# Attention and a binary feed-forward block on one core: dense pieces dealt to other steps, relu sums joined, constants cast on ScalarE, and the PSUM banks divided 2-3-2

## The chip, the cores and the metric

The kernel runs on one core of one Trainium2 chip. The metric is the device time of one execution in microseconds (us). A core has TensorE (PE, its weight loads are PEld), VectorE (DVE), ScalarE (ACT), GpSimd (POOL) and SyncE (SP), which issues most of the transfers. PE writes into PSUM, which has eight banks of 128 x 512 f32; here seven of them are lent to units of work and the eighth, o_bank, collects the attention output.

## What is computed

The input x is 8 batches of 1024 tokens with 256 channels. Weights and constants of other layers of the reference are left out here.

```python
# attention in windows of (b, n); in the kernel one batch is 1024 tokens, 16 heads of 16 channels
qkv = x @ w_qkv.T + b_qkv
q, k = elu(q) + 1, elu(k) + 1
q, k = apply_rope(q, sin, cos), apply_rope(k, sin, cos)
attn = softmax(q @ k.T * D**-0.5) @ v
attn = attn + depthwise_conv3(v, w_lepe) + b_lepe
h0 = layernorm(x + attn)
# feed-forward, the three kernels are booleans read as +1 or -1
h = relu(s0 * (concat[h0, -h0] @ pm1(k0))) * 2
h = relu(s1 * (h @ pm1(k1))) * 2
out = layernorm(h0 + s2 * (h @ pm1(k2)))
```

## The kernel before, in words

**Steps.** The work is 8 batches (NB), each of 8 pairs of heads (PAIRS), each of 8 blocks of 128 keys (T): 512 steps of one pair and one key block, 64 to a batch (BATCH). In step s, PE computes the scores S of step s + 12 for two heads in two halves (`scores`, L527 to L535: four matmuls into banks), and the transposed scores T of step s (`scores_T`, L537 to L545: four matmuls); S and T of different heads are issued in turns and run side by side on different rows of the array. DVE takes the row maxima of S (`row_max`, L889), ACT takes exp of T (`exp_probs`, L737), and PE multiplies the exponentials of step s - 1 with v (`weighted_v`, L573, 16 matmuls). The maxima of a pair are joined, transposed by PE in the step with kt = 5 ("max rows", L590) and written by SP into the query stack before T of that pair begins. In the step with kt = 2 the attention output of the pair before is transposed ("O rows", L596).

**Dense pieces.** All the rest of PE's work is cut in units that each fill one PSUM bank and that are dealt by hand to steps, in `dealt` (L106): for batch c the projections of q and k ("proj", 4 units each), the bounds of the heads ("scale", 2), the projection of v ("V", 4); for batch m, one batch behind, the transposes of the normed rows ("hT", 2 + 2), the first layer ("L0", 8 + 8 units, two to a step), the second ("L1", 8 + 8 units, each of two pieces in two steps) and the third ("L2", 2 + 2 units, two pieces each). A piece is issued in a step between the two groups of scores. A "scale" unit is eight small matmuls (`head_bounds`, L554): four sums of relu outputs, each used in two products. What does not fit in the steps is done behind them, in the order of END_UNITS (L101).

**Order on ACT and DVE.** Both follow the same table in their own streams. For a step ACT does the two exps of the second head, then what ended at the end of the step before (`done_behind(s - 1)`, for proj), then what ended within this step, then the two exps of the first head, then the ReLU of the hidden unit that ended last in this step (`done_behind(s)`). DVE does the two maxima of the first head of S, then `done_behind(s - 1)`, the max rows, the rest of this step's units, the norm's statistics, and the other two maxima (L1084 to L1121). A hidden unit is read twice, by ACT (the high half in f16, L804) and then by DVE (the low half, L959), and its bank is free after DVE. A proj unit's bank is free after ACT's second read (L782).

**Banks.** `program_order` (L179) hands out banks in rings: a unit takes the next bank of its kind's ring, and PE waits (`wait_free`) until the unit that had this bank before has been read. "O rows" and "max rows" units take a bank of the dense ring as well, ahead of the step's dense pieces. In the first batch the rings are S (0, 1, 4), T (2, 3, 5) and dense (6); from the second batch on S (0, 1), T (2, 3), dense (4, 5, 6).

**The start and the constants.** Before step 0, q and k of batch 0 are projected, rotated, split, written to HBM and read back as stacks, and the maxima of 12 steps are taken (L1041). Then DVE works out the signs and scales of the feed-forward kernels (L1060 to L1069, nine small operations in a chain) and, behind the maxima of steps 0 to 5, casts k0, k1 and k2 from bytes to f16 (`weights`, L1071). The bytes of k1 lie in the tile attn (stage1, L341).

**GpSimd and SP.** POOL does, for each batch in a written order (L1281 to L1308), the normalisation of the attention of each pair, the depthwise convolution (lepe), the elu, rotation and split of q and k of the next batch with their writes to HBM, the scales of the norms and the load of x. SP waits in its order for the max rows, the freed stacks and the scratch, and issues the loads, the stores of the output (L515) and the loads of the edges and of xT (L517).

Of the kernel before, what the change touches and what calls it, by code (L numbers as in the profile page):

```python
# [24 lines left out]
ALU = mybir.AluOpType  # L25
# [75 lines left out]
END_UNITS = [*out_units(TAIL - 1, 1), *hT_units(TAIL, 0), *hT_units(TAIL, 1),  # L101
# [4 lines left out]
def dealt():  # L106
# [9 lines left out]
    for c in range(1, NB):  # L116
        b = (c - 1) * BATCH
        deal(b + Q_AT, proj_units(c, 0))
        deal(b + SCALE_AT[0], [("scale", c, 0)])
        deal(b + K_AT, proj_units(c, 1))  # L120
        deal(b + SCALE_AT[1], [("scale", c, 1)])
        deal(b + V_AT, v_units(c))
    for m in range(NB - 1):
        b = (m + 1) * BATCH
        deal(b + 17, hT_units(m, 0), 2)
        deal(b + 18, hT_units(m, 1), 2)
        deal(b + 19, hidden_units("L0", m, 0), 2)
        if m < TAIL - 1:
            deal(b + 23, hidden_units("L1", m, 0, range(3)))
            deal(b + 33, hidden_units("L1", m, 0, range(3, KF)))  # L130
            deal(b + 47, hidden_units("L0", m, 1), 2)
            deal(b + 51, out_units(m, 0))
            deal(b + 55, hidden_units("L1", m, 1))
            deal(b + 75, out_units(m, 1))
        else:
            deal(b + 23, hidden_units("L1", m, 0))
            deal(b + 39, hidden_units("L0", m, 1), 2)
            deal(b + 43, out_units(m, 0))
            deal(b + 47, hidden_units("L1", m, 1))
# [39 lines left out]
def program_order():  # L179
# [26 lines left out]
    rings = (4, 5, 6, 0, 1, 2, 3)  # L206
# [74 lines left out]
def build(nc, x, xT, wT, b_qk, b_v, w_lepe, b_lepe, cos, sin, k0, k1, k2, s0, s1, s2, out):  # L281
    with ExitStack() as ctx:
# [33 lines left out]
        relu_sum = sb("relu_sum", [P, 4, 2], F32)  # L316
        pow2_q = sb("pow2_q", [P, 1 + H], F32)
# [23 lines left out]
        stage1 = attn[:].rearrange("p t c -> p (t c)").bitcast(U8)  # L341
# [44 lines left out]
        max_split = sem("max_split")  # L386
        scale_made = sem("scale_made")
# [47 lines left out]
        def _(sp):  # L435
# [74 lines left out]
            for n in range(NB * PAIRS):  # L510
# [16 lines left out]
        def _(pe):  # L527
# [26 lines left out]
            def head_bounds(unit):  # L554

                w = unit[2]
                pe.wait_ge(dve_setup, 3)
                units.wait_read(pe, ("proj", unit[1], 2 * w + 1, 1))
                units.wait_free(pe, unit)
                bank = units.out(unit)  # L560
                terms = [(ct, half) for ct in (2 * w, 2 * w + 1) for half in range(2)]
                for ct, half in terms:
                    total = relu_sum[:, ct, half:half + 1]
                    nc.tensor.matmul(bank[:, 0:1], same_head[:], total, start=(ct, half) == terms[0],  # L564
                                     stop=(ct, half) == terms[-1], skip_group_check=True)
                for ct, half in terms:
                    total = relu_sum[:, ct, half:half + 1]
                    done = nc.tensor.matmul(bank[:, 1:1 + H], total.to_broadcast([P, P]), head_mask[:],  # L568
                                            start=(ct, half) == terms[0], stop=(ct, half) == terms[-1],
                                            skip_group_check=True)  # L570
                done.then_inc(units.full_sem(unit), 1)
# [164 lines left out]
        def _(act):  # L736
# [69 lines left out]

            def normalise(m, which, t):
# [24 lines left out]
            for s in range(STEPS):  # L832
# [9 lines left out]
                if kt == 3 and n > 0 and j != 5 and n + 3 < NB * PAIRS:  # L842
                    copy_v(n + 2 if j == 6 else n + 3)
                if kt == 5 and j == 6 and n + 3 < NB * PAIRS:
                    copy_v(n + 3)
# [14 lines left out]
                if b >= 1 and i in NORMALISE_AT[0]:  # L860
                    normalise(b - 1, 0, NORMALISE_AT[0][i] + 1)
                if j == 5 and 3 <= kt < 7 and b + 1 < NB:
# [5 lines left out]
            copy_o_rows(NB * PAIRS - 1)  # L868
            for t in range(T // 2):
                normalise(NB - 1, 0, t)  # L870
            for unit in END_UNITS:
# [9 lines left out]
        def _(dve):  # L881
# [36 lines left out]
            def elu(c, ct):  # L918
# [4 lines left out]
                  .then_inc(elu_done, 1)  # L923

# [91 lines left out]
            for ct in range(2):  # L1016
                elu(0, ct)
            dve.wait_ge(rows_loaded, 7 * 16)
# [3 lines left out]
            def rotated(ins):  # L1022
                ops[0] += 1
                ins.then_inc(start_split, 1)
                if ops[0] in (2, 4):
                    elu(0, 1 + ops[0] // 2)
                dve.wait_ge(start_split, ops[0])
# [13 lines left out]
            for v in range(T + LEAD):  # L1041
                if v == T + 1:
                    split_max_rows(0)
                for h in range(2):
                    for half in range(2):
                        row_max(v, h, half)
                if v == T - 1:
# [310 lines left out]
```

## Time and profile before

| | us |
|---|---|
| median of 3 runs | 2267.48 (2260.52 to 2269.52) |
| profiled execution | 2269.32 |
| its span, first to last instruction | 2267.5 |
| around the span | 1.8 |

| engine | busy us | share of the span |
|---|---|---|
| PE matmul | 2133.7 | 94% |
| DVE | 1685.9 | 74% |
| ACT | 1475.4 | 65% |
| POOL | 913.3 | 40% |

Busy time of PE is modelled from pipelined matmuls, and two matmuls that run side by side count once. Where a step begins can be read from the first of its four matmuls of line L543: a step is four of them, a batch 256.

### The profile page before, as it was taken

What the parts mean: (1) busy time and instruction counts of PE and PEld (TensorE: products, weight loads), DVE (VectorE), ACT (ScalarE), POOL (GpSimd) and SP (SyncE); (2) the same over time, 40 slices, a digit from 0 to 9 for tenths busy, and PEclk for the clock granted to TensorE, in tenths of its full rate; (3) what the DMA queues carried; (4) which work ended last, traced back from release to release, by engine and by line L of the source; (5) the groups of instructions that cost most, each with busy time, mean ns of one, the idle gap of its engine ahead of it and who ended that gap; (6) DMA issues with size and microseconds to landing.
All of it is one profiled execution on the core that took longest, in us unless ns stands there. A gap on an engine that the chain in (4) does not pass through costs nothing.

```text
span 2267.5 us, 43445 instructions
## 1 busy us (share of the span) xinstructions
PE 2133.7 (94%) x17088; PEld 869.2 (38%) x17088; DVE 1685.9 (74%) x3018; ACT 1475.4 (65%) x2845; POOL 913.3 (40%) x522
## 2 busy tenths in 40 slices
PE   4788899999999999999999999999999999899997
PEld 2122323344343444334343443434443343334344
DVE  6957687878787877878777787868778787878243
ACT  3157578766677666866677666776668666776631
POOL 1228608560375406851185603853067601600000
PEclk8579899999999999999999999999999999999999
DMA  5001110011001110012000210011101110010000
GB/s 176 27 8 39 48 45 16 27 52 39 15 9 52 54 32 13 25 45 67 15 15 29 69 39 15 9 52 61 31 9 34 36 48 15 16 34 1 1 19 19
DMA packets 40140, 76.87 MB, mean 34 GB/s; under 512 B 14992, under 2 KB 19456, under 8 KB 36864
## 3 DMA queue, kind: packets, MB, share of 16 engines
q1 hardware_dynamic: 34752, 51.02, 7.9%
q0 software_dynamic: 5184, 23.07, 2.8%
q8 instruction: 135, 2.21, 0.4%
q14 instruction: 69, 0.57, 0.1%
HBM read 46.27 MB, written 25.17 MB: 32 GB/s over the span
## 4 chain that ended last, share of the span: by engine, by line
PE 81%; DVE 13%; ACT 4%; issue 1%; DMA 1%; POOL 0%; SPq 0%; ACTq 0%; POOLq 0%; DVEq 0%
PE unit_banks L656 24%; PE unit_banks L533 20%; PE o_bank L586 20%; DVE maxima L892 9%; PE unit_banks L613 5%; PE unit_banks L669 5%; PE unit_banks L624 3%; ACT probs L745 2%; PE unit_banks L601 1%; PE unit_banks L543 1%; PE unit_banks L564 1%; PE unit_banks L568 1%; DVE h0T L959 1%; ACT rows L812 0%; PE unit_banks L594 0%
## 5 line engine op out<-in xcount | busy, mean ns | idle before, releaser
L892 DVE TENSOR_REDUCE maxima<-unit_banks 128x1 f32<-128x512 f32 x2048 | 1308.6, 685 | 428.9 <-PE unit_banks L533 422.1
L745 ACT ACTIVATE probs<-unit_banks 128x512 f32<-128x512 f32 x2048 | 1116.0, 598 | 665.4 <-PE unit_banks L543 655.1
L533 PE MATMUL unit_banks<-k_stack,q_stack 48*128 48x512 f16 x2048 | 662.2, 394 | 61.8 <-DVE maxima L892 38.3
L543 PE MATMUL unit_banks<-q_stack,k_stack 50*128 50x512 f16 x2048 | 651.2, 389 | 1.9 <-ACT probs L745 1.7
L586 PE MATMUL o_bank<-probs,v_pair 128*32 128x256 f32 x8192 | 570.1, 391 | 3.1 <-issue 3.1
L656 PE MATMUL unit_banks<-h0T,w 128*128 128x512 f16 x2048 | 480.9, 380 | 0.0
L1217 POOL TENSOR_TENSOR attn<-o_rows_sb,rden 128x256 f32<-128x256 f32 x63 | 39.0, 618 | 923.2 <-DVE rden L905 912.6
L533 PEld LDWEIGHTS unit_banks<-k_stack,q_stack 48*128 48x128 f16 x2048 | 154.5, 94 | 597.8 <-DVE maxima L892 300.0
L586 PEld LDWEIGHTS o_bank<-probs,v_pair 128*32 128x32 f32 x8192 | 208.8, 109 | 308.7 <-issue 217.4
L656 PEld LDWEIGHTS unit_banks<-h0T,w 128*128 128x128 f16 x2048 | 186.5, 98 | 228.1 <-issue 38.6
L543 PEld LDWEIGHTS unit_banks<-q_stack,k_stack 50*128 50x128 f16 x2048 | 153.3, 94 | 16.1 <-ACT probs L745 11.4
L613 PE MATMUL unit_banks<-xT_sb,wT_sb 128*128 128x512 f32 x256 | 131.2, 642 | 24.0 <-DMA xT_sb<-in_xT 9.7
L959 DVE SCALAR_TENSOR_TENSOR h1T<-unit_banks,h1T 128x512 f16<-128x512 f32 x128 | 87.4, 683 | 81.5 <-ACT h1T L804 81.5
L1233 POOL TENSOR_TENSOR lepe_tmp<-v_ext,lepe_rows 128x1024 f32<-128x1024 f32 x48 | 113.0, 2354 | 70.6 <-DVE max_rows L913 68.1
L669 PE MATMUL unit_banks<-w,h1T 128*128 128x256 f16 x1024 | 121.2, 273 | 8.0 <-DVE rows L977 8.0
L656 PE MATMUL unit_banks<-hT,w 128*128 128x512 f16 x512 | 122.8, 380 | 4.9 <-DVE h0T L959 4.4
L1189 POOL TENSOR_SCALAR work<-work 128x1024 f32<-128x1024 f32 x26 | 72.0, 2767 | 112.5 <-ACT work L782 111.3
L1235 POOL TENSOR_TENSOR rows<-rows,lepe_tmp 128x1024 f32<-128x1024 f32 x48 | 113.1, 2357 | 3.8
L804 ACT ACTIVATE h1T<-unit_banks 128x512 f16<-128x512 f32 x128 | 77.3, 604 | 52.1 <-PE unit_banks L656 52.1
L669 PEld LDWEIGHTS unit_banks<-w,h1T 128*128 128x128 f16 x1024 | 97.0, 98 | 27.7 <-DVE rows L977 8.9
L959 DVE SCALAR_TENSOR_TENSOR h0T<-unit_banks,h0T 128x512 f16<-128x512 f32 x128 | 86.5, 684 | 11.4 <-ACT h0T L804 10.9
L812 ACT ACTIVATE rows<-rows,shift,rstd 128x256 f32<-128x256 f32 x120 | 71.1, 603 | 20.7 <-POOL shift L1255 20.7
(125 smaller groups left out, 1541.7 us busy)
## 6 DMA issues: line engine op xcount, KB each, us to landing
rows<-in_x POOLq DMA_DIRECT2D x8, 1024.0 KB, 7.6
xT_sb<-in_xT SPq DMA_DIRECT2D x8, 1024.0 KB, 14.2
q_stack<-q_scratch SPq DMA_DIRECT2D x128, 64.0 KB, 2.0
k_stack<-k_scratch SPq DMA_DIRECT2D x128, 64.0 KB, 2.0
out<-rows SPq DMA_DIRECT2D x8, 1024.0 KB, 4.1
q_scratch<-parts POOLq DMA_DIRECT2D x14, 512.0 KB, 3.3
k_scratch<-parts POOLq DMA_DIRECT2D x14, 512.0 KB, 3.3
q_stack<-q_scratch SPq DMA_DIRECT2D x128, 32.0 KB, 1.9
```

Of the source, the lines that this page charges most:

```text
L533: nc.tensor.matmul(units.out(unit), q_stack[row:row + STACK, r, t * P:(t + 1) * P], k_stack[row:row + STACK, r, half * 512:(half + 1) * 51 ...
L543: nc.tensor.matmul(units.out(unit), k_stack[row:end, r, kt * P:(kt + 1) * P], q_stack[row:end, r, half * 512:(half + 1) * 512], start=True ...
L586: done = nc.tensor.matmul(o, v_pair[:, n % RING, kt, h, :], p[:, :, parity, :], start=kt == 0 and half == 0, stop=kt == T - 1, skip_group_ ...
L613: done = nc.tensor.matmul(units.out(unit), wT_sb[:, kc, ct * P:(ct + 1) * P], xT_sb[:, kc, half * 512:(half + 1) * 512], start=kc == 0, st ...
L656: done = nc.tensor.matmul(units.out(unit), w, a, start=k == 0 and i == 0, stop=k == tiles - 1 and i == 1)
L669: done = nc.tensor.matmul(units.out(unit)[:, t * C:(t + 1) * C], h1T[:, a, k, (2 * i + t) * P:(2 * i + t + 1) * P], w2[:, k, :], start=k = ...
L745: nc.scalar.activation(probs[:, 2 * (kt % 2) + h, half * 512:(half + 1) * 512], units.out(unit), ACT.Exp, scale=exp_regs[2 * (n % PAIRS) + ...
L804: done = nc.scalar.activation(dst[:, 0, unit[3], :], units.out(unit), ACT.Relu)
L892: nc.vector.reduce_max(maxima[:, v // T % 2, h * T + t, half:half + 1], units.out(unit), AXIS_X)\
L959: free(unit, nc.vector.scalar_tensor_tensor(dst[:, 1, u, :], s, 0.0, dst[:, 0, u, :], ALU.max, ALU.subtract))
L1233: ins = combine(lepe_tmp[:], v_ext[:, t + tap:t + tap + T // 2, :], row(tap), ALU.mult)
L1235: ins = combine(base, base, lepe_tmp[:], ALU.add)
```

## The change

- `rings` is one setting for all steps: S (0, 1), T (2, 3, 4), dense (5, 6). The ring of the start and of the end is reordered.
- `dealt` has other steps: q at 6 (7 before), scale at 14 (12) and 40 (35), k at 32 (29; 22 for batch 1, its scale at 28), V at 50 (43), hT at 19 and 20 (17, 18), L0 at 22 (19) and 46 (47), L1 of the first half at 26 and 36 (23, 33), L2 at 54 (51), L1 of the second half at 58 for six units and 74 for two (55), L2 at 79 (75). The last L1 unit of batch 6 goes behind the steps (LATE_UNITS).
- DVE sums the four relu sums to one (`join_sums`), and a scale unit is two matmuls instead of eight.
- The scales and w0 are made on DVE ahead of the first maxima; w1 and w2 are cast on ACT, one operation of 128 x 512 at the end of each of steps 8 to 27 (16 for w1, 4 for w2). The bytes of k1 lie in rows[1].
- The copies of v for the pairs, the statistics, the normalisation on ACT, the order on POOL and two steps on SP are moved along.

```diff
-Q_AT, K_AT, V_AT, SCALE_AT = 7, 29, 43, (12, 35)
-STATS_AT = {**{6 + t // 2: (0, t - t % 2) for t in range(0, T, 2)}, 14: (1, 4), 16: (1, 6), 52 + 4: (1, 0), 52 + 6: (1, 2)}
-MOMENTS_AT = {10: 0, 17: 1}
-NORMALISE_AT = ({13: 0, 14: 2, 15: 4, 16: 6}, {20 + t: t for t in range(T)})
-COPY_V_AT = {3: 3}
+Q_AT, V_AT = 6, 50
+K_AT, SCALE_AT = {1: 22}, ({}, {1: 28})
+STATS_AT = {**{6 + t // 2: (0, t) for t in range(0, T, 2)}, 27: (1, 4), 29: (1, 6), 59: (1, 0), 61: (1, 2)}
+MOMENTS_AT = {10: 0, 31: 1}
+NORMALISE_AT = ({13: 0, 14: 2, 15: 4, 16: 6}, {37 + t: t for t in range(T)})
+COPY_V_AT = {3: (0, 1, 2, 3, 4, 7), 1: (7,), 5: (7,)}
+WEIGHTS_AT = 8
...
+LATE_UNITS = [("L1", TAIL - 1, 1, KF - 1), *out_units(TAIL - 1, 1)]
+END_UNITS = [*LATE_UNITS, *hT_units(TAIL, 0), *hT_units(TAIL, 1),
...
-        deal(b + 17, hT_units(m, 0), 2)
-        deal(b + 18, hT_units(m, 1), 2)
-        deal(b + 19, hidden_units("L0", m, 0), 2)
+        deal(b + 19, hT_units(m, 0), 2)
+        deal(b + 20, hT_units(m, 1), 2)
+        deal(b + 22, hidden_units("L0", m, 0), 2)
         if m < TAIL - 1:
-            deal(b + 23, hidden_units("L1", m, 0, range(3)))
-            deal(b + 33, hidden_units("L1", m, 0, range(3, KF)))
-            deal(b + 47, hidden_units("L0", m, 1), 2)
-            deal(b + 51, out_units(m, 0))
-            deal(b + 55, hidden_units("L1", m, 1))
-            deal(b + 75, out_units(m, 1))
+            deal(b + 26, hidden_units("L1", m, 0, range(3)))
+            deal(b + 36, hidden_units("L1", m, 0, range(3, KF)))
+            deal(b + 46, hidden_units("L0", m, 1), 2)
+            deal(b + 54, out_units(m, 0))
+            deal(b + 58, hidden_units("L1", m, 1, range(6)))
+            deal(b + 74, hidden_units("L1", m, 1, range(6, KF)))
+            deal(b + 79, out_units(m, 1))
...
-    rings = {"S": (0, 1, 4), "T": (2, 3, 5), "": (6, 0, 1, 2, 3, 4, 5)}
+    rings = {"S": (0, 1), "T": (2, 3, 4), "": (5, 6, 4, 0, 1, 2, 3)}
...
-    rings[""] = (6,)
+    rings[""] = (5, 6)
...
-        if s == BATCH:
-            rings = {"S": (0, 1), "T": (2, 3), "": (4, 5, 6)}
...
-    rings = (4, 5, 6, 0, 1, 2, 3)
+    rings = (5, 6, 4, 0, 1, 2, 3)
...
-                if j == 3 and b >= 2:
+                if j == 5 and b >= 2:
                     store_out(b - 2)
-                if j == 5 and b < NB - 1:
+                if j == 6 and b < NB - 1:
                     load_edges(b + 1)
...
-                terms = [(ct, half) for ct in (2 * w, 2 * w + 1) for half in range(2)]
-                for ct, half in terms:
...
+                bank, total = units.out(unit), sums[:, w:w + 1]
+                nc.tensor.matmul(bank[:, 0:1], same_head[:], total, start=True, stop=True, skip_group_check=True)
+                nc.tensor.matmul(bank[:, 1:1 + H], total.to_broadcast([P, P]), head_mask[:], start=True, stop=True,
+                                 skip_group_check=True).then_inc(units.full_sem(unit), 1)
...
+                if i < 2 * KF:
+                    k, cols = i // 2, slice(i % 2 * 512, (i % 2 + 1) * 512)
+                    nc.scalar.activation(w1[:, k, cols], k1_u8[:, k, cols], ACT.Identity, bias=s_work[:, 2:3],
+                                         scale=s_work[:, 1:2])
+                else:
+                    k = slice(2 * (i - 2 * KF), 2 * (i - 2 * KF) + 2)
+                    nc.scalar.activation(w2[:, k], k2_u8[:, k], ACT.Copy, bias=-1.0, scale=2.0)
...
+            def join_sums(c, w):
+
+                units.wait_read(dve, ("proj", c, 2 * w + 1, 1))
+                nc.vector.reduce_sum(sums[:, w:w + 1], relu_sum[:, 2 * w:2 * w + 2, :], AXIS_XY).then_inc(sums_joined, 1)
...
                 lepe(b, 7, LEPE_OPS)
+                if b == 0:
+                    normalise_o(n)
                 if b + 1 < NB:
                     elu(b + 1, 0)
-                if b >= 2:
-                    ln_scales(b - 2, 1)
                 normalise_o(n + 1)
...
                 normalise_o(n + 2)
+                if b >= 2:
+                    ln_scales(b - 2, 1)
+                if b > 0:
+                    normalise_o(n + 3)
...
```

## Rows read from the trace of the kernel before

**Rows 1.** The page, part 4: the chain that ended last, by engine.

```profile
PE 81%; DVE 13%; ACT 4%; issue 1%; DMA 1%; POOL 0%; SPq 0%; ACTq 0%; POOLq 0%; DVEq 0%
```

**Rows 2.** Windows of four batches, L543 alone: us, busy (count), PEclk.

```profile
86.40:334.20 247.80, 90.69 (x256) 19.88 (x256) 0.86 0.11 33
334.20:585.80 251.60, 82.65 (x256) 19.64 (x256) 0.99 0.11 32
585.80:848.80 263.00, 79.42 (x256) 19.07 (x256) 1.00 0.11 34
...
1902.50:2154.40 251.90, 80.34 (x256) 18.54 (x256) 1.00 0.05 14
```

**Rows 3.** Windows of steps of batch 2, L543 alone, columns as there.

```profile
634.27:640.01 5.74, 1.22 (x4) 0.30 (x4) 1.00 0.01 3
649.78:655.90 6.12, 2.77 (x8) 0.66 (x8) 1.00 0.20 50
655.90:665.18 9.28, 2.92 (x8) 0.67 (x8) 1.00 0.06 11
706.07:722.10 16.03, 4.88 (x16) 1.18 (x16) 1.00 0.13 35
748.04:755.90 7.86, 2.44 (x8) 0.59 (x8) 1.00 0.19 69
759.83:764.24 4.41, 1.22 (x4) 0.30 (x4) 1.00 0.04 15
```

**Rows 4.** Timeline of PE, step 13 of batch 2: start us, us, what.

```profile
640.57 0.28 PE L594 MATMUL unit_banks<-ident,max_both 128*16 128x128 f32 x1
642.45 1.92 PE L669 MATMUL unit_banks<-w,h1T 128*128 128x256 f16 x16 [1.60 <-DVE rows L977]
```

**Rows 5.** Timeline of DVE, step 13 of batch 2.

```profile
640.44 1.29 DVE L892 TENSOR_REDUCE maxima<-unit_banks 128x1 f32<-128x512 f32 x2 [0.25 <-PE unit_banks L533]
641.64 0.74 DVE L977 SCALAR_TENSOR_TENSOR rows<-unit_banks,s_work,rows 128x512 f32<-128x512 f32 x1
```

**Rows 6.** Timeline of PE, step 21 of batch 2.

```profile
673.90 1.03 PE L656 MATMUL unit_banks<-hT,w 128*128 128x512 f16 x4
675.56 1.04 PE L656 MATMUL unit_banks<-hT,w 128*128 128x512 f16 x4 [0.63 <-DVE h0T L959]
```

**Rows 7.** Timeline of PE, step 50 of batch 2.

```profile
793.47 2.13 PE L656 MATMUL unit_banks<-hT,w 128*128 128x512 f16 x8
```

**Rows 8.** Timeline of PE, a projection in batch 0.

```profile
220.75 1.96 PE L613 MATMUL unit_banks<-xT_sb,wT_sb 128*128 128x512 f32 x4 [2.33 <-ACT h1T L782]
```

**Rows 9.** Windows of L543: batch 0, steps 0-6 and 56-63; batch 1, 0-6.

```profile
86.40:121.50 35.10, 13.91 (x28) 2.62 (x28) 0.61 0.06 16
312.53:334.30 21.77, 10.60 (x32) 2.68 (x32) 1.00 0.10 23
334.30:354.40 20.10, 10.01 (x28) 2.44 (x28) 1.00 0.07 18
```

**Rows 10.** Timeline of DVE at the start, in order of time.

```profile
58.01 19.23 DVE L892 TENSOR_REDUCE maxima<-unit_banks 128x1 f32<-128x512 f32 x32 [7.71 <-PE unit_banks L533]
...
87.64 2.26 DVE L1061 TENSOR_SCALAR s_sign<-s_sign 128x3 f32<-128x3 f32 x1
...
118.68 1.20 DVE L1082 TENSOR_SCALAR w<-rows 128x2048 f16<-128x2048 uint8 x1
```

**Rows 11.** Lines: ACT with scale and bias from tiles.

```profile
L812 ACT ACTIVATE rows<-rows,shift,rstd 128x256 f32<-128x256 f32 x120 | 71.1, 603 | 20.7 <-POOL shift L1255 20.7
```

**Rows 12.** Waits of SP: what, us in total, times, longest.

```profile
SPq L278 <- DMA k_scratch<-parts: 145.2, 7, 24.9
```

**Rows 13.** Timeline behind the last step: PE.

```profile
2157.01 7.15 PE L669 MATMUL unit_banks<-w,h1T 128*128 128x256 f16 x64
...
2168.87 3.53 PE L636 MATMUL unit_banks<-ident,rows 128*128 128x128 f32 x16 [4.71 <-ACT rows L812]
```

**Rows 14.** Window of L543 in batch 3, columns as in rows 2.

```profile
911.40:930.00 18.60, 6.79 (x19) 1.46 (x18) 0.91 0.09 22
```

More of the change, by code:

```diff
@@ L118, in dealt @@
         deal(b + Q_AT, proj_units(c, 0))
[L119 to L121 removed]
+        deal(b + scale_at(c, 0), [("scale", c, 0)])
+        deal(b + k_at(c), proj_units(c, 1))
+        deal(b + scale_at(c, 1), [("scale", c, 1)])
         deal(b + V_AT, v_units(c))
@@ L316, in build @@
         relu_sum = sb("relu_sum", [P, 4, 2], F32)
+        sums = sb("sums", [P, 2], F32)
         pow2_q = sb("pow2_q", [P, 1 + H], F32)
@@ L554, in head_bounds @@
             def head_bounds(unit):
-                w = unit[2]
+                _, c, w = unit
                 pe.wait_ge(dve_setup, 3)
-                units.wait_read(pe, ("proj", unit[1], 2 * w + 1, 1))
+                pe.wait_ge(sums_joined, 2 * c + w + 1)
                 units.wait_free(pe, unit)
-                bank = units.out(unit)
-                terms = [(ct, half) for ct in (2 * w, 2 * w + 1) for half in range(2)]
-                for ct, half in terms:
[L563 to L571, printed above, removed]
+                bank, total = units.out(unit), sums[:, w:w + 1]
+                nc.tensor.matmul(bank[:, 0:1], same_head[:], total, start=True, stop=True, skip_group_check=True)
+                nc.tensor.matmul(bank[:, 1:1 + H], total.to_broadcast([P, P]), head_mask[:], start=True, stop=True,
+                                 skip_group_check=True).then_inc(units.full_sem(unit), 1)
             def weighted_v(s, half):
@@ L841, in _ @@
                     copy_o_rows(n - 1)
[L842 to L845, printed above, removed]
+                if n > 0 and j in COPY_V_AT.get(kt, ()):
+                    ahead = {1: 1, 3: 2, 5: 3}[kt] if j == PAIRS - 1 else 3
+                    if n + ahead < NB * PAIRS:
+                        copy_v(n + ahead)
                 for unit in done_within(s):
@@ L868, in _ @@
             copy_o_rows(NB * PAIRS - 1)
+            high_part(LATE_UNITS[0])
             for t in range(T // 2):
                 normalise(NB - 1, 0, t)
-            for unit in END_UNITS:
+            for unit in END_UNITS[len(LATE_UNITS):]:
                 if unit[0] in HIDDEN:
@@ L1017, in _ @@
                 elu(0, ct)
+            join_sums(0, 0)
             dve.wait_ge(rows_loaded, 7 * 16)
@@ L1026, in rotated @@
                     elu(0, 1 + ops[0] // 2)
+                if ops[0] == 4:
+                    join_sums(0, 1)
                 dve.wait_ge(start_split, ops[0])
@@ L1040, in _ @@
             v_out(("V", 0, 3))
[L1041 to L1047, printed above, removed]
-                    join_maxima(0)
             dve.wait_ge(k_loaded, 6 * 16)
@@ L1095, in _ @@
                         split_max_rows(unit[1])
+                for w, at in enumerate((Q_AT, k_at(b + 1))):
+                    if b + 1 < NB and i == at + 5:
+                        join_sums(b + 1, w)
                 if kt == RECIPROCAL_STEP and n > 0:
@@ L1119, in _ @@
                         join_maxima(v // T)
-                if s < 6:
-                    weights(s)
+            for unit in done_behind(STEPS - 1):
+                dense(unit)
             final, m = NB * PAIRS - 1, NB - 1
@@ L1149, in _ @@
             ln_moments(m, 0)
-            for unit in END_UNITS[:2]:
+            for unit in LATE_UNITS:
                 dense(unit)
-            units.wait_read(dve, END_UNITS[1])
+            units.wait_read(dve, LATE_UNITS[-1])
             normalise(0)
@@ L1156, in _ @@
             ln_moments(m - 1, 1)
-            for unit in END_UNITS[2:]:
+            for unit in END_UNITS[len(LATE_UNITS):]:
                 dense(unit)
@@ L1302, in _ @@
                     rotate_side(b + 1, 1)
-                normalise_o(n + 3)
+                if b == 0:
+                    normalise_o(n + 3)
                 if b + 1 < NB:
                     split(b + 1, 1)
+                normalise_o(n + 4)
+                normalise_o(n + 5)
+                if b + 1 < NB:
                     load_x(b + 1)
-                for k in range(4, PAIRS - 1):
-                    normalise_o(n + k)
+                normalise_o(n + 6)
             ln_scales(NB - 1, 0)
```

43 lines of the change are left out of this document (26 added, 17 removed).

## The prediction, made before the changed kernel ran

> **What bounds the kernel now.** I read the chain first: PE carries 81% of it and DVE 13% [rows 1]. Then I asked how long a batch of 64 steps takes, by counting the 256 matmuls of L543: 263.0 us in batches 2 to 6 (batch 3: 264.6), 251.6 in batch 1, 251.9 in batch 7, 247.8 in batch 0, where the clock was granted to 0.86 only [rows 2]. Then single steps: a step with an L0 or L1 piece takes 3.93 us (7.86 for two), one with a proj or V piece 4.01 (16.03 for four), O rows add 0.48 (4.41), a scale unit adds 1.8 (5.74), a step with no piece takes 3.06, the two hT steps together 9.28 [rows 3]. In the full steps PE is never free, so whatever makes it wait there is paid in full. The question is therefore which waits for a bank the new rings make.
>
> **How a bank wait looks.** PE can begin a piece some 0.5 us into a step. DVE reads what ended with the step before only after two maxima of this step. In step 13 of batch 2 the L2 unit has the bank of the one that ended in step 12: max rows start at 640.57, L2 could start 0.1 later, starts at 642.45 [rows 4], when the residual, issued behind the maxima at 641.64, has been written [rows 5]. That is 1.8 us lost, and with no max rows ahead 1.85. Two more waits of a shorter kind are there: the second L0 unit of a step waits for the second of the step before, 0.83 us in step 21 (second group of four at 675.56, due 0.83 behind 673.90) [rows 6]; in step 50 the pieces take 2.13 instead of 1.90 behind O rows, and the step is 0.43 longer than 3.93 + 0.04 + 0.48 [rows 7]. Without something ahead this kind costs 0.91. A unit behind a proj unit waits for ACT, which does two exps and two activations first: 2.33 us [rows 8].
>
> **What the rings do.** I went through the table of steps with both rings, own units (O rows, max rows) included, and counted the units whose bank is freed only in the very step in which they want it. Before, with three dense banks, a steady batch has 5 (two of them hidden, by the scale unit ahead and in the hT steps). After, with two, it has 23: every O rows or max rows unit that takes a turn hands the next dense unit the bank of the last one. By kind, for batches 2 to 6:
> first piece, step kt = 6 or 3, nothing ahead (steps 6, 14, 19, 30, 38, 46, 62): 7 x 1.83 = 12.8;
> first piece behind O rows (2, 26, 42, 50, 58): 5 x (1.81 - 0.48) = 6.7;
> behind O rows and a proj bank (10, 34): 2 x (2.35 - 0.48) = 3.7;
> V behind V in step 53: 1.8; behind the new scale unit in step 40: 1.4;
> second L0 unit (23, 24, 25, 47, 48, 49): 6 x 0.91 = 5.5; second hT unit (20): 1.3.
> Sum 33.2 us a batch. Batch 1 has 18 (24.3 us), batch 7 has 19 (22.8 us): 152 waits and 213 us in all, 1.40 each. None of them has a cover: PE issues in order, and all that stands behind it are the scores that ACT and DVE wait for.
>
> **What it saves in the steady batches.** Three old waits go: 1.77 + 0.85 + 0.43 = 3.05. Two scale units of eight small matmuls become two: 6/8 of 1.8, twice, 2.7. The sum on DVE (a few tenths, twice a batch) lies beside PE. One of the two empty steps is filled: an empty step takes 3.06 for 2.1 of PE work (3.93 less the piece's 1.83), so 0.95. The hT steps keep 6.4 of PE work out of 9.28 less O rows 0.48: 2.4. Together 9.1; after: 263.0 - 9.1 + 33.2 = 287.1, +24.1 a batch, +120.5 in five, less 1.6 for batch 3's half-clock stretch. Batch 1: -10.6 (three pieces go to later steps, 3.1; scale 4.3; old waits 1.3; hT steps 1.9) + 24.3 = +13.7. Batch 7: one more piece in place of an empty step +0.9, old waits -1.3, hT steps -2.4, new waits +22.8: +20.0.
>
> **Batch 0.** Here PE has room, and one dense bank made each proj and V unit wait for the last. With two banks only V in step 53 does. S loses its third bank: with S on three banks an empty step takes 2.72 (21.77 for 8), on two 2.87 (20.10 for 7) [rows 9]; I take 2.80, since that batch 1 has other work too. w1 and w2 on ACT: an ACT operation with scale and bias from tiles takes 603 ns for 256 columns [rows 11], so some 0.8 for 512; ACT's four exps leave about 0.4 free in a step, 20 steps lose 0.2: 4. Sum: 50 x 2.80 + 4 + 12 x 4.01 + 1.8 + 2 x 3.25 = 200.5. Steps 0 to 6 took 35.1 at a clock of 0.61 [rows 9], and 0.14 of the whole batch's clock was lost [rows 2], which cost at most 35; the new batch keeps PE busier, I take 11 (between 0 and 35). 211.5 against 247.8: -36.3. T's third bank is costed at nothing: ACT was the last to free a T bank in few steps.
>
> **Start.** DVE idles 7.7 us before its first maxima at 58.0, and the constants took it from 87.6 to 119.9 between maxima [rows 10]. The nine small operations and w0 come to 10.4; moved ahead they fill the 7.7 and delay the maxima by 2.7. Their old price is inside batch 0.
>
> **Costed at nothing.** The tail: PE ends L2 at 2164.2 and waits to 2168.9 for the normed rows [rows 13]; the late L1 unit's 3.7 fits in these 4.7. The K chain on POOL starts three steps later; SP waited 20.7 us a batch for the k scratch [rows 12], to about step 44. Now it is step 47, with SP's loads of the max rows that PE asks for in step 48 queued behind; one step is left. If that cover goes, each step of lateness costs 4.5 us in six batches. The store and the edges on SP move by one or two pairs and had a step or more to spare; POOL's norm scales move too, on an engine that is busy 40% of the span.
>
> **Sum.** 120.5 - 1.6 + 13.7 + 20.0 - 36.3 + 2.7 = +119.0 on the span of 2267.5: 2386.5, with 1.8 around it 2388.3. The profiled execution (2269.3) is 1.8 above the median, so against the runs I forecast 2387, 5% slower.
>
> **Rivals.**
> *The clock falls as well.* The trace shows it where PE has light steps in a row: in batch 3 the stretch with steps 16 to 19 has 0.91 of the clock [rows 14], and cost 1.6, in one of six equal batches. The new waits bunch in steps 19 to 26 and 46 to 50, where a fifth to a quarter of PE's time is idle; against it, batch 0's empty steps, 2.72 for 2.1 of work, ran at 1.00 [rows 9]. Four such falls a batch in seven batches at 1.6: +45, 2432. Chance 0.14. The Trainium skill (TensorE: Matmul & The Clock Gate, A second HAM failure mode: psum-queue depth-cycling) says that a matmul stream that cycles through PSUM banks and idles briefly between groups makes the clock swing between its two levels; by that rule this is the likelier outcome, but the trace has it once in six batches.
> *Not slower: the bank waits shrink.* If DVE and ACT, rested by the first waits, free the banks sooner, each may cost what the cheapest one did, 0.43: 152 x 0.43 = 65 against savings of 94 (213 - 119), 2240. It decides below 94/152 = 0.62 each. Against it: the two maxima of the same step stand ahead of the read in DVE's stream, however rested it is [rows 5]. Chance 0.04.
> *A second buffer is enough.* With all waits hidden the sum is 2269.3 - 94, 2175. Speaks for it: nothing but that two banks suffice when units are read within a step. Chance 0.01. The Trainium skill (TensorE: Matmul & The Clock Gate, HAM oscillation — how this bites in real kernels) tells of a kernel in which double-buffering PSUM gave no further gain; by that the number of dense banks would hardly matter. The 1.8 us of step 13 say otherwise here.
> *The K chain is late.* Two steps late in six batches, +54 on top: 2441. Chance 0.03. *The sum of scale units is left as it was* (the compiler does not drop anything here, but the four relu sums might be late for join_sums): +2.7 a batch, inside the range.
>
> **Numbers.** Forecast 0.76, clock 0.14, K chain 0.03, not slower 0.05, elsewhere 0.02. A measurement of this kernel can tell 0.5% (11 us) from no change. Faster 0.05, within 0.01, slower 0.94. Range: the low end has waits 15% cheaper (-32) and batch 0 without any clock loss (-11), with a little for both: 2340. The high end takes in the clock's case: 2435.
>
> **What would show it.** Steady batches of 287 us by the count of L543; in them steps 6, 30, 38, 62 at 5.8 and steps 23 to 25 at 4.8, with PE released by DVE's L959 or L977; scale steps at 0.45 above the piece; proj steps of batch 0 at about 4.0; DVE with no gap before the first maxima and ACT casting in steps 8 to 27. I am wrong if a batch stays at 263 or below, if PE's waits for DVE or ACT ahead of dense pieces stay below 100 us in all, or if batch 0 does not shrink.

## The result, and the profile after

The changed kernel takes 2442.82 us (median of 4 runs, 2431.28 to 2448.98), the kernel before 2266.13 beside it. The ratio is 1.078, with a 95% interval of 1.073 to 1.082. The profiled execution, the longest of the four, has a span of 2447.2. The forecast was 2387 with a range of 2340 to 2435: the direction holds and so do the waits for banks, but the median lies 8 us above the range, and most of what is missing is a second cause, the clock of TensorE. Of all the executions below one, of the run read_first, took 5119.74 us where its other nine took 2255.87 to 2268.51; nothing on record says why, and the ratios leave it out.

The chain that ended last, by engine and by line, in the changed kernel:

```profile
PE 76%; DVE 19%; ACT 2%; issue 2%; DMA 1%; SPq 0%; POOL 0%; ACTq 0%; POOLq 0%; DVEq 0%
PE unit_banks L660 23%; PE unit_banks L545 20%; PE o_bank L590 19%; DVE maxima L911 13%; PE unit_banks L673 5%; PE unit_banks L617 5%; PE unit_banks L628 2%; DVE h1T L983 2%; DVE h0T L983 1%; ACT probs L749 1%; PE unit_banks L555 1%; PE unit_banks L640 1%; DVE hT L980 0%; ACT work L786 0%; DVE rows L1001 0%
```

PE has gone from 81% of the chain [rows 1] to 76%, and DVE from 13% to 19%. Lines are numbered anew: S is L545, T is L555, the dense pieces L660 and L673, the low half on DVE L983. Next, who waits for whom (us in total, times, longest us); these groups were small or absent before:

```profile
PEld unit_banks L660 <- DVE h1T L983: 81.8, 48, 2.0
...
PE unit_banks L660 <- DVE h1T L983: 69.5, 47, 1.7
PEld unit_banks L660 <- DVE h0T L983: 62.9, 49, 1.7
...
PE unit_banks L660 <- DVE h0T L983: 40.9, 49, 1.5
```

PE itself (not its weight loads, which wait over the same time) now stands 69.5 + 40.9 us before pieces of L1 and L0 until DVE has read a bank, 96 times, and the modelled ends of matmuls hide a part of each wait. Now the batches, as in [rows 2], from batch 0 on with 5, 6 left out (window, us, busy and count of L555, PEclk):

```profile
90.63:298.83 208.20, 93.18 (x256) 21.64 (x256) 0.96 0.13 38
298.83:565.63 266.80, 82.44 (x256) 19.72 (x256) 0.99 0.10 30
565.64:864.76 299.12, 80.61 (x256) 18.73 (x256) 0.96 0.10 30
864.77:1159.46 294.69, 79.93 (x256) 18.83 (x256) 0.98 0.10 31
1159.47:1458.59 299.12, 80.71 (x256) 18.82 (x256) 0.96 0.10 30
2052.46:2326.70 274.24, 80.24 (x256) 18.36 (x256) 0.99 0.04 12
```

Batch 0 is 39.6 us shorter. Batches 1 and 7 are 15 and 22 longer, and batches 2 to 6, which took 263.0, take 294.7 to 299.1. In these the clock stands at 0.96 to 0.98, where it had been 1.00 (0.99 in batch 3 for one fall). Single steps of batch 4 (steps 2, 23 to 25, 30, 34 and 38):

```profile
1167.32:1173.06 5.74, 1.22 (x4) 0.29 (x4) 1.00 0.01 3
1265.42:1280.05 14.63, 3.71 (x12) 0.89 (x12) 1.00 0.20 63
1297.67:1305.04 7.37, 1.29 (x4) 0.31 (x4) 0.77 0.01 1
1316.99:1324.93 7.94, 1.65 (x4) 0.32 (x4) 0.79 0.01 2
1336.88:1342.62 5.74, 1.22 (x4) 0.29 (x4) 1.00 0.02 4
```

Step 2 takes 5.74 for 4.41, steps 23 to 25 take 4.88 each for 3.93, step 38 takes 5.74: at full clock these are the waits of the prediction, 1.33, 0.95 and 1.81. Step 30 is of the same kind as 38, and step 34 is a wait behind a proj unit in a step with O rows, priced at 6.36; but they take 7.37 and 7.94, at a clock of 0.77 and 0.79. That is the part that was not in the sum. All falls of batches 1 to 7 begin in steps with a wait for a bank (6, 10, 14, 19, 30, 34, 38, 62). One plain wait, step 38, in the timeline (start us, us, what):

```profile
1336.78 0.60 ACT L808 ACTIVATE h1T<-unit_banks 128x512 f16<-128x512 f32 x1
...
1337.31 1.29 DVE L911 TENSOR_REDUCE maxima<-unit_banks 128x1 f32<-128x512 f32 x2 [0.25 <-PE unit_banks L545]
1337.34 1.08 ACT L749 ACTIVATE probs<-unit_banks 128x512 f32<-128x512 f32 x2
...
1338.52 0.68 DVE L983 SCALAR_TENSOR_TENSOR h1T<-unit_banks,h1T 128x512 f16<-128x512 f32 x1
...
1339.26 1.90 PE L660 MATMUL unit_banks<-h0T,w 128*128 128x512 f16 x8 [1.75 <-DVE h1T L983]
```

ACT writes the high half of the L1 unit at 1336.78, before this step's maxima are even begun. DVE takes the two maxima until 1338.6 and only then reads the unit. The new unit could have begun at 1337.5, where PE's idle time starts, and begins at 1339.26.

### The profile page after: what moved, and what is told of

Read it like the earlier page. It is cut to its first block, busy times and chain, and to the rows that moved or that the text cites. A ratio compares the mean times of both kernels' runs of the same rounds, so it can differ in the third digit from the quotient of the medians.

```text
span 2447.2 us, 43069 instructions
## 1 busy us (share of the span) xinstructions
PE 2166.0 (89%) x16896; PEld 851.5 (35%) x16896; DVE 1683.0 (69%) x3029; ACT 1491.5 (61%) x2865; POOL 913.2 (37%) x522
## 4 chain that ended last, share of the span: by engine, by line
PE 76%; DVE 19%; ACT 2%; issue 2%; DMA 1%; SPq 0%; POOL 0%; ACTq 0%; POOLq 0%; DVEq 0%
PE unit_banks L660 23%; PE unit_banks L545 20%; PE o_bank L590 19%; DVE maxima L911 13%; PE unit_banks L673 5%; PE unit_banks L617 5%; PE unit_banks L628 2%; DVE h1T L983 2%; DVE h0T L983 1%; ACT probs L749 1%; PE unit_banks L555 1%; PE unit_banks L640 1%; DVE hT L980 0%; ACT work L786 0%; DVE rows L1001 0%
## 5 line engine op out<-in xcount | busy, mean ns | idle before, releaser
L545 PE MATMUL unit_banks<-k_stack,q_stack 48*128 48x512 f16 x2048 | 671.1, 397 | 58.2 <-DVE maxima L911 29.7
L555 PE MATMUL unit_banks<-q_stack,k_stack 50*128 50x512 f16 x2048 | 658.0, 392 | 1.2 <-ACT probs L749 1.2
L660 PE MATMUL unit_banks<-h0T,w 128*128 128x512 f16 x2048 | 499.6, 391 | 82.7 <-DVE h1T L983 57.8
L545 PEld LDWEIGHTS unit_banks<-k_stack,q_stack 48*128 48x128 f16 x2048 | 155.6, 94 | 606.6 <-DVE maxima L911 314.2
L660 PEld LDWEIGHTS unit_banks<-h0T,w 128*128 128x128 f16 x2048 | 189.1, 100 | 327.3 <-DVE h1T L983 68.1
L660 PE MATMUL unit_banks<-hT,w 128*128 128x512 f16 x512 | 129.4, 385 | 46.6 <-DVE h0T L983 32.8
L555 PEld LDWEIGHTS unit_banks<-q_stack,k_stack 50*128 50x128 f16 x2048 | 153.8, 94 | 13.4 <-ACT probs L749 7.8
L983 DVE SCALAR_TENSOR_TENSOR h1T<-unit_banks,h1T 128x512 f16<-128x512 f32 x128 | 87.4, 683 | 82.1 <-ACT h1T L808 82.0
L1250 POOL TENSOR_TENSOR lepe_tmp<-v_ext,lepe_rows 128x1024 f32<-128x1024 f32 x48 | 113.1, 2357 | 73.2 <-DVE max_rows L932 70.7
L673 PE MATMUL unit_banks<-w,h1T 128*128 128x256 f16 x1024 | 127.2, 281 | 2.7 <-DVE h1T L983 2.7
L1252 POOL TENSOR_TENSOR rows<-rows,lepe_tmp 128x1024 f32<-128x1024 f32 x48 | 113.1, 2355 | 3.8
L673 PEld LDWEIGHTS unit_banks<-w,h1T 128*128 128x128 f16 x1024 | 99.0, 101 | 30.7 <-issue 13.5
L983 DVE SCALAR_TENSOR_TENSOR h0T<-unit_banks,h0T 128x512 f16<-128x512 f32 x128 | 86.4, 686 | 28.1 <-ACT h0T L808 28.1
L808 ACT ACTIVATE h0T<-unit_banks 128x512 f16<-128x512 f32 x128 | 76.9, 606 | 22.5 <-PE unit_banks L660 19.4
```

Of the source, the lines that this page charges most:

```text
L545: nc.tensor.matmul(units.out(unit), q_stack[row:row + STACK, r, t * P:(t + 1) * P], k_stack[row:row + STACK, r, half * 512:(half + 1) * 51 ...
L555: nc.tensor.matmul(units.out(unit), k_stack[row:end, r, kt * P:(kt + 1) * P], q_stack[row:end, r, half * 512:(half + 1) * 512], start=True ...
L660: done = nc.tensor.matmul(units.out(unit), w, a, start=k == 0 and i == 0, stop=k == tiles - 1 and i == 1)
L673: done = nc.tensor.matmul(units.out(unit)[:, t * C:(t + 1) * C], h1T[:, a, k, (2 * i + t) * P:(2 * i + t + 1) * P], w2[:, k, :], start=k = ...
L808: done = nc.scalar.activation(dst[:, 0, unit[3], :], units.out(unit), ACT.Relu)
L983: free(unit, nc.vector.scalar_tensor_tensor(dst[:, 1, u, :], s, 0.0, dst[:, 0, u, :], ALU.max, ALU.subtract))
```

## The experiments

**dense3: the dense work gets the third bank back.**

```diff
-    rings = {"S": (0, 1), "T": (2, 3, 4), "": (5, 6, 4, 0, 1, 2, 3)}
+    rings = {"S": (0, 1), "T": (2, 3), "": (5, 6, 4, 0, 1, 2, 3)}
...
-    rings[""] = (5, 6)
+    rings[""] = (4, 5, 6)
```

> The changed kernel with T on banks 2 and 3 and the dense work on 4, 5 and 6, in all steps; nothing else differs. Theory (the dense bank waits cost some 33 us a steady batch, and the clock falls that follow from PE's idle time another 10): all of it goes, steady batches of 254 us, 2181 us in all. Rival (the new placement makes its own light steps, and the clock falls come from these): the waits go but the falls stay, steady batches of 264, about 2235.

It took 2221.18 us, 0.981 of the kernel before (0.979 to 0.982), and 40 more than expected. Batch 3, and batch 5:

```profile
807.29:1067.07 259.78, 79.05 (x256) 19.08 (x256) 1.00 0.11 35
1326.86:1590.52 263.66, 79.73 (x256) 19.03 (x257) 0.99 0.11 34
```

So one bank, moved from T to the dense work, is worth 222 us, and all else in the change, the rings of batch 0 included, makes the kernel 2% faster. Batch 3 is 259.8, not 254; the clock is at 1.00 in four of the five batches 2 to 6, so the many falls do not come from the new placement's light steps. Of the 5.8 too many, 1.4 stands in step 47: the next step's first scores wait for the max rows.

```profile
1002.58 0.39 PE L545 MATMUL unit_banks<-k_stack,q_stack 48*128 48x512 f16 x1 [1.35 <-DMA q_stack<-max_rows]
```

This is the late K chain of the rivals, in a small way: SP holds the load of the max rows behind the stack that needs the k scratch. In the changed kernel the longer steps hid it: PE never waits for the max rows there. In batch 5 the same wait is followed by the only fall of batches 2 to 6, and steps 47 and 48 take 6.54 and 6.84 instead of 5.34 and 3.91. Step 46 still waits 0.95 for a bank, steps 22, 26 and 50 are 0.2 to 0.4 longer than their pieces, and the rest, some 2.7 by subtraction, must stand in the light steps 14 and 19 to 21.

**t2_d2: T loses its third bank, dense stays at two.**

```diff
-    rings = {"S": (0, 1), "T": (2, 3, 4), "": (5, 6, 4, 0, 1, 2, 3)}
+    rings = {"S": (0, 1), "T": (2, 3), "": (5, 6, 4, 0, 1, 2, 3)}
```

> The changed kernel with T on banks 2 and 3; dense stays on 5 and 6, and bank 4 is not used in the steps. Theory (T's third bank is worth nothing in any stage): 2443 within 10 us, steady batches of 295 to 299, batch 0 at 208. Rival (the third bank lets ACT lag behind in the steps with elu and casts): batch 0 longer by 5 to 10 us and steady batches by 3 or more, 2460 or above.

2441.17 us against 2442.82: no difference that can be measured, and batch 0 is 209.6 against 208.2. So T's third bank is worth nothing that these runs can tell. Batch 3 has five falls here:

```profile
860.32:1156.49 296.17, 80.87 (x256) 18.80 (x256) 0.97 0.10 31
```

Batches 2 to 6 take 291.5 to 296.3, with 6.8 or 17.1 us of each at half clock.

**own_bank: O rows and max rows take no turn in the dense ring.** On t2_d2:

```diff
             if h == 0:
                 for u in own_units(s):
-                    yield u, rings[""], True, True
+                    yield u, (4,), True, True
```

> As the run before, but O rows and max rows units have bank 4 for themselves and take no turn in the dense ring. Theory (most long waits come about because these units take a turn): by the table of steps 10 waits of 23 are left in a steady batch, six of them the short 0.95 of the second L0 unit; 264 us a batch, hardly a clock fall, 2245 in all. Rival (two banks are too few for the dense units by themselves): 285 or more a batch, 2400.

2260.48 us, 15 more than expected and 181 less than t2_d2. Batch 3 at 265.8, with the clock at 1.00:

```profile
814.71:1080.54 265.83, 78.67 (x256) 19.06 (x256) 1.00 0.11 34
```

What costs is less that the dense units have two banks than that the 16 small units of a batch take turns with them: each hands the next dense unit the bank that the last one has just filled. When the small units have a third bank for themselves, dense units on two banks wait only in the L0 steps, in step 20 and behind the scale unit in step 40. These waits, of 1.4 us at most, brought no fall in batches 2 to 6.

**rings_only: the new rings in the kernel before, nothing else.**

```diff
-    rings = {"S": (0, 1, 4), "T": (2, 3, 5), "": (6, 0, 1, 2, 3, 4, 5)}
+    rings = {"S": (0, 1), "T": (2, 3, 4), "": (5, 6, 4, 0, 1, 2, 3)}
...
-    rings[""] = (6,)
+    rings[""] = (5, 6)
...
-        if s == BATCH:
-            rings = {"S": (0, 1), "T": (2, 3), "": (4, 5, 6)}
...
```

> The kernel before with nothing but the new rings. Theory (the rings alone make it slower): 25 waits in a steady batch, 296 to 303 us with the clock falls, batch 0 shorter by 25 to 35, about 2470 in all. Rival (the new placement is what costs): less than 2330.

2497.53 us (two runs, 1.101 to 1.106 of before), 27 more than expected. The rings alone do it, and in the old placement they do more. The first seven steps of batch 0, then batches 3 and 4:

```profile
92.57:127.80 35.23, 13.72 (x28) 2.54 (x28) 0.63 0.04 11
897.79:1198.48 300.69, 79.94 (x256) 18.92 (x256) 0.97 0.10 30
1198.49:1501.55 303.06, 79.79 (x256) 18.98 (x256) 0.96 0.10 30
```

The first seven steps still take 35.2 us; in the changed kernel, with the constants out of DVE's way, they take 23.6:

```profile
90.63:114.25 23.62, 12.58 (x28) 2.34 (x28) 0.76 0.07 17
```

Batch 0 as a whole is 222.0 here, against 247.8 before and 208.2 in the changed kernel: 26 of the 40 saved there come with the rings, the other 14 with the constants, the placement and the joined sums.

**filler: PE is kept busy while it waits.** On t2_d2, 4, 6 or 8 junk matmuls into the idle bank 4 ahead of each late unit of batches 1 to 7, a little less than its wait:

```diff
...
             def dense(unit, part):
+                if part == 0:
+                    for _ in range(late.get(unit, 0)):
+                        nc.tensor.matmul(unit_banks[:, 4, :], w0[:, 0, 0:P], w0[:, 0, 0:512], start=True, stop=True,
+                                         skip_group_check=True)
```

> The kernel t2_d2 (2441 us) with PE kept busy where it waits for a dense bank: ahead of each late unit of batches 1 to 7, 4, 6 or 8 matmuls of 512 columns write junk into the idle bank 4, a little less than the wait. Theory (the clock falls because PE idles in these waits, and the falls cost 4 to 12 us a batch on top of them): steady batches of 285 to 288, the clock at full speed in them, 2390 to 2400 in all. Rival (the falls come from the light steps 14 and 19 to 21 or from something other than idle PE): the falls stay, and the fillers add, 2440 or more.

2402.74 us (1.058 to 1.062 of before), 38 less than t2_d2 with 892 matmuls more, and 3 above the expected 2390 to 2400. Batches 3 and 4, and step 30 of batch 4:

```profile
853.74:1142.02 288.28, 78.61 (x256) 19.01 (x256) 1.00 0.10 32
1142.02:1430.30 288.28, 78.61 (x256) 19.00 (x256) 1.00 0.10 31
1274.21:1279.94 5.73, 1.22 (x4) 0.30 (x4) 1.00 0.01 1
```

The clock is at 1.00 in all of batches 1 to 7, every batch from 2 to 6 takes 288.3, and step 30 takes 5.73 where it had 7.37. Nothing that PE waits for has changed, only what it does meanwhile. So the falls come from the idle waits themselves. They cost (1486.8 - 1441.4) = 45 us in these five batches of the changed kernel's profiled execution, which has 99 us of them at half clock. In that of t2_d2, from which this run differs by the filling alone, they cost 1471.7 - 1441.4 = 30 us, with 65 at half clock. What is left, 288.3, is within 1.2 us of the steady batch of the prediction (287.1).

**read_first: DVE reads the finished unit ahead of the two maxima.**

```diff
-                if v < STEPS:
-                    for half in range(2):
-                        row_max(v, 0, half)
                 for unit in done_behind(s - 1):
                     dense(unit)
+                if v < STEPS:
+                    for half in range(2):
+                        row_max(v, 0, half)
```

> The changed kernel, but DVE reads what ended with the step before ahead of the first two maxima instead of behind them. Theory (a long wait is two maxima and one read on DVE; without the maxima ACT's read of the same unit is the last): long waits fall from 1.8 to some 1.0, the short ones from 0.95 to a few tenths, those for ACT behind a proj unit stay; with fewer clock falls steady batches of 268 to 278, 2320 to 2370. Rival (the read is not what the waits hang on, or the maxima that come later hold PE up just as long): 2430 or more.

2261.87 us (0.997 to 0.999 of before): 181 less than the changed kernel, for one move of two lines, and 58 below the low end of what was expected (2320). Batch 3, and the start of its step 38:

```profile
810.62:1076.75 266.13, 79.55 (x256) 19.55 (x256) 1.00 0.11 34
```

```profile
968.47 0.60 ACT L808 ACTIVATE h1T<-unit_banks 128x512 f16<-128x512 f32 x1
...
969.11 0.69 DVE L983 SCALAR_TENSOR_TENSOR h1T<-unit_banks,h1T 128x512 f16<-128x512 f32 x1 [0.35 <-ACT h1T L808]
969.71 1.28 DVE L911 TENSOR_REDUCE maxima<-unit_banks 128x1 f32<-128x512 f32 x2
...
969.86 1.90 PE L660 MATMUL unit_banks<-h0T,w 128*128 128x512 f16 x8 [0.66 <-DVE h1T L983]
```

DVE reads the unit as soon as ACT has, at 969.11, and the new unit starts at 969.86, 1.28 into the step instead of 2.37. A long wait is 0.72 now (4.65 for 3.93), a short one of L0 0.05; those behind a proj unit stay (6.36 in step 34), as they hang on ACT. In the full steps the maxima that come later hold nothing up (3.92 in step 27). Some waits are left, the longest of 1.8 and 1.9 in steps 10 and 34, and batches 5 and 6 have one fall and two, in steps 14 and 34.

**sums_only: only the joined relu sums, in the kernel before.**

```diff
...
-                for ct, half in terms:
-                    total = relu_sum[:, ct, half:half + 1]
-                    nc.tensor.matmul(bank[:, 0:1], same_head[:], total, start=(ct, half) == terms[0],
...
+                bank, total = units.out(unit), sums[:, w:w + 1]
+                nc.tensor.matmul(bank[:, 0:1], same_head[:], total, start=True, stop=True, skip_group_check=True)
...
```

> The kernel before with nothing but the joined relu sums (and the first scale unit in step 13 instead of 12, so that the sum is there). Theory (each scale unit is 1.35 us shorter on PE, but the one in step 35 and the one in step 13 stand ahead of units that wait for a bank, so most of it turns into a longer wait): about 1.8 us a steady batch, 2250 to 2255. Rival (all of it counts): 19 us, 2245.

2250.49 us, 0.993 (0.992 to 0.995). A steady batch takes 261.2, 1.8 less, as expected; steps 12 and 13, then step 35:

```profile
879.17:888.93 9.76, 2.44 (x8) 0.59 (x8) 1.00 0.01 2
973.52:979.26 5.74, 1.22 (x4) 0.30 (x4) 1.00 0.00 0
```

Step 35 takes 5.74 as before: of the scale unit's 1.8 only 0.45 is left, and the L1 unit behind it waits for its bank until the same moment. Step 13 hides its scale unit in the old wait for L2. Of the rest, in the profiled execution, batch 0 is 236.2 for 247.8, with 40.5 instead of 68.4 us at half clock, and batch 1 is 247.2 for 251.5. The two spans differ by 25 us and the medians by 16, so part of this is the difference between one execution and another.

**best and best_read_first: versions that beat both kernels.** The changed kernel with S (0, 1, 4), T (2, 3), dense (5, 6) in batch 0, then S (0, 1), T (2, 3), dense (4, 5, 6), and

```diff
...
+        if s == BATCH:
+            rings = {"S": (0, 1), "T": (2, 3), "": (4, 5, 6)}
...
-                load_freed_stack(n)
+                if j == 5:
+                    load_freed_stack(n - 1)
+                if j != 4:
+                    load_freed_stack(n)
...
                 for t in tiles(half):
                     ln_stats_of(m, 0, t)
+                if half == 0:
+                    dense(LATE_UNITS[0])
...
-            for unit in LATE_UNITS:
+            for unit in LATE_UNITS[1:]:
```

> The changed kernel with S (0, 1, 4), T (2, 3), dense (5, 6) in batch 0 and S (0, 1), T (2, 3), dense (4, 5, 6) from batch 1; DVE reads the late L1 unit between the statistics of the two halves at the end; SP loads the stack of pair 8 behind the max rows of pair 6. Theory: against dense3 (2221) the start is 3 to 4 us shorter (S on three banks), batch 0 by 3 to 5, the wait of 1.4 for max rows in step 47 goes (6 batches, 8), the end is 2 to 4 shorter: 2200 to 2208. Rival (the start is bound by DVE and the end by the norm's chain, whatever the banks and the order): 2213 or more.

2194.64 us, 0.968 (0.967 to 0.970), 27 less than dense3 and below the expected 2200 to 2208. Step 0 starts at 85.6 instead of 91.2, batches 1 and 3 are

```profile
290.52:533.15 242.63, 82.20 (x256) 19.89 (x256) 1.00 0.11 33
791.59:1050.02 258.43, 79.11 (x256) 19.15 (x256) 1.00 0.11 35
```

and the wait for max rows is gone (3.93 in step 47), as is every fall in batches 1 to 7. The end behind the last scores is 116.5 instead of 118.8. Then DVE's read was put first in this kernel, too:

> The kernel best (2195) with DVE reading what ended with the step before ahead of the first two maxima. Theory (the read behind the maxima costs PE something only where a unit wants that bank in the same step; with three dense banks that is steps 19 and 46, and smaller delays in 26 and 50): 1 to 3 us a steady batch, 2180 to 2192. Rival (reading first helps as much as it did with two banks, or its later maxima now cost more than it gives): below 2150, or above 2200.

2186.73 us, 0.966 (0.964 to 0.968); batch 3:

```profile
784.10:1041.53 257.43, 79.94 (x256) 19.87 (x256) 1.00 0.11 35
```

With a third dense bank the order on DVE is worth 1.0 us a batch, where it had been worth some 30. It matters only where a unit wants the bank in the step in which it is read: step 46 falls from 4.88 to 3.92, but the light step 14 grows from 3.32 to 3.79.

## Why the prediction was right, and where it was wrong

**The bank waits: right, in kind and place, and nearly in size.** The forecast had the steady batch at 287.1 without clock falls; with the falls taken out by filler it is 288.3. That this is met to 1.2 us is in part luck, for two misses cancel: the third dense bank takes away 29.9 us (288.3 against 258.4 in best), where the waits were priced at 33.2, and what is left is 258.4 and not 253.9. The sizes of most kinds came out near what was priced: 1.81 in step 38, 1.33 in step 2, 0.95 in steps 23 to 25, 1.87 in step 34 (6.36 in read_first and in batch 3 of the changed kernel for 4.01 + 0.48). Steps 14 and 19 were priced at 1.83 each, and with the falls out they are only 1.2 and 0.6 longer than in dense3. Three batch lengths where no fall or few come in were met to 2%: batch 1 266.8 (265.2), batch 7 274.2 (271.8), batch 0 208.2 (211.5). That T's third bank is worth nothing measurable is shown by t2_d2.

**The clock: wrong, and this is the step that failed.** Of the 60.7 us between the span of 2386.5 in the sum and the 2447.2 measured, 51.3 lie in batches 2 to 6, and 45 of these are the clock (30 in the profiled execution of t2_d2, and 38 between the medians of t2_d2 and filler). The sum put this term at nothing in the steady batches. The prediction held the case for a rival with a chance of 0.14, because it had counted one fall in six batches (batch 1, at 0.99 in [rows 2], has one more), and because the light steps of batch 0 ran at full clock with as much idle time. That comparison was the error. In the light steps (56 to 63 of batch 0) no idle piece of PE is longer than 0.93 us; here the idle time comes in single waits of 1.3 to 1.9 us, several within a few steps (10 and 14; 30, 34 and 38). By the profile PE is idle for a tenth of the time in both (busy 19.6 of 21.8 us, and 267.8 of 299.1 in batch 4). This sets two stretches side by side; no run varied the length of the waits alone.

The trace of the kernel before had the better comparison, in another stretch of batch 0. There PE waits for the one dense bank, 1.76, 1.85 and 1.76 us ahead of V units and max rows, and the clock is at 0.76:

```profile
262.00:290.60 28.60, 6.38 (x18) 1.10 (x18) 0.76 0.26 88
```

The changed kernel spends 13.7 or 23.9 us of each of batches 2 to 6 at half clock, in 4 to 7 falls, and one costs some 1.6. The rule of the Trainium skill that was set beside this rival (TensorE: Matmul & The Clock Gate, A second HAM failure mode: psum-queue depth-cycling) is that short idle times between groups of matmuls that go through the banks in turn make the clock swing. The trace agrees: PE waits for banks between groups of matmuls, and its clock falls 4 to 7 times a batch. The rival's time, 2432, is 11 below the result, and the range ended at 2435, since I had cut it close above that rival.

**The rival "not slower": rightly held unlikely, and one move away.** The argument against it was that the maxima stand ahead of the read in DVE's stream. That is so, and read_first shows that this order makes the waits long (0.72 instead of 1.81): with the read first, and the falls gone with the waits but for a few, the changed kernel on its two dense banks is as fast as the kernel before, though still 41 us behind dense3. **The rival "a second buffer is enough"** fell, and even with the order changed or the small units out of the ring the kernel takes 2262 and 2260, not 2175.

**The start: near by accident.** The nine small operations took 1.7 us and not 7.3, so DVE is ready early:

```profile
49.53 0.16 DVE L1077 TENSOR_SCALAR s_sign<-s_in 128x3 f32<-128x3 f32 x1
...
51.27 2.29 DVE L1087 TENSOR_TENSOR w<-rows 128x2048 f16<-128x2048 uint8 x1
...
57.44 22.16 DVE L911 TENSOR_REDUCE maxima<-unit_banks 128x1 f32<-128x512 f32 x32 [3.09 <-PE unit_banks L545]
```

The first maxima start at 57.44. But S has two banks now instead of three, and the first 32 maxima take 22.2 us for 19.2 [rows 10]. Step 0 starts at 90.6, 4.2 later, for the 2.7 priced. In best, with three banks, these maxima take 19.2 again, and step 0 starts at 85.6:

```profile
57.12 19.22 DVE L916 TENSOR_REDUCE maxima<-unit_banks 128x1 f32<-128x512 f32 x32 [3.06 <-PE unit_banks L550]
```

**The tail: wrong by 7.3.** It was costed at nothing, as 3.7 us of matmuls fit in 4.7 of idle time. What was missed is a wait on another engine's order, the same kind as in the steps:

```profile
2329.79 3.62 PE L660 MATMUL unit_banks<-h0T,w 128*128 128x512 f16 x16
...
2333.64 2.70 DVE L1016 BATCH_NORM_STATS2 stats<-rows 128x6 f32<-128x256 f32 x8
...
2336.94 0.66 DVE L983 SCALAR_TENSOR_TENSOR h1T<-unit_banks,h1T 128x512 f16<-128x512 f32 x1
...
2337.66 7.30 PE L673 MATMUL unit_banks<-w,h1T 128*128 128x256 f16 x50 [2.73 <-DVE h1T L983]
...
2339.51 2.07 ACT L828 ACTIVATE rows<-rows,shift,rstd 128x256 f32<-128x256 f32 x4 [5.48 <-POOL shift L1272]
...
2344.79 1.04 PE L640 MATMUL unit_banks<-ident,rows 128*128 128x128 f32 x8
```

PE finishes the late L1 unit at 2333.4. DVE reads it behind all statistics and moments, at 2336.94, and L2 waits for that to 2337.66; then the clock falls, L2 takes 7.3 us for the 50 matmuls that are left, and the transposes start at 2344.79, 3.2 after ACT had the normed rows ready (2341.6). This is half of the 7.3. The rest follows behind: DVE norms its rows only after it has read L2, so PE waits 1.39 and 2.16 more, and the next 32 matmuls of the first layer take 8.75 for 7.07, at a second fall. In best, where DVE reads the late unit ahead of the second half's statistics, the end is 2.3 shorter than in dense3.

**The K chain: right, and hidden.** Nothing of it shows in the changed kernel. In the faster dense3 it costs 1.4 us a batch, so the cover of one step that the prediction saw was real, and thin.

**The savings: half of what was priced in a steady batch.** The sum had 9.1 us; best, which has no wait for max rows, takes 258.4 for 263.0, so 4.6. A scale unit costs 0.45 above its step, as priced (4.38 for 3.93 in step 40 of dense3), but sums_only shows that one in front of a bank wait saves little by itself. The rest is missing in step 46, in steps 22, 26 and 50 and in the light steps 14 and 19 to 21. Over the whole, dense3 gains 2% where the sum without waits had 4%. Of its 44.9 us, 39.0 come from batch 0, and by rings_only most of that comes with the rings (26 of 40) and not with the placement, the sums or the constants; batches 1 to 6 give 18, and batch 7, a start of 91.2 for 86.5 and a tail of 118.8 for 113.1 take back 12.

## What to carry to other kernels

Count, for each unit of work, in which step its buffer is freed and in which it is wanted, and count the small units that take turns in the same ring, since one of them makes two buffers into one. Where both fall in one step, the wait is set by what stands ahead of the freeing read in that engine's stream, so try the order there before spending a buffer. When a wait is put on TensorE, price the clock as well: single waits of 1.3 to 1.9 us, some steps apart, brought it down again and again, though in the light steps of batch 0 the same idle share in pieces below 1 us had not.

## What the runs showed of the hardware

- Junk matmuls in the waits made the kernel 38 us faster (2441 to 2403), by the clock alone.
- Which waits bring a fall on differs between batches of the same instructions: batches 3 and 5 of the changed kernel take 294.7, with 13.7 us at half clock, and batches 2, 4 and 6 take 299.1, with 23.9.
- Three of the nine tiny operations (128x3 or 128x1) took 1.8 to 2.3 us each before, behind the first maxima (2.26 at 87.64 [rows 10]), and 0.16 to 0.17 each when moved ahead of them. Each of the three long ones ends within 0.05 us of an operation of GpSimd (89.90 beside 89.86, then 92.29 beside 92.28 and 94.71 beside 94.70); when they were moved ahead, GpSimd did nothing at that time. So they seem to wait for GpSimd, but no run isolates it. The first of its three operations, in the kernel before:

```profile
87.52 2.34 POOL L1235 TENSOR_TENSOR rows<-rows,lepe_tmp 128x1024 f32<-128x1024 f32 x1
```
